# Causal mask added by VectorE in PSUM instead of by TensorE products, in a macaron transformer block

## The reference

```
q, k = rope(q), rope(k)
scores = einsum(q, k) * 64 ** -0.5
scores = where(tril, scores, -inf)
probs = softmax(scores)
out = einsum(probs, v) -> wo
```

## Time and profile before

| | |
|---|---|
| median of 3 runs | 1355.13 us (1354.36 to 1357.69) |
| profiled execution, own time | 1354.49 us |
| its span, first to last instruction | 1352.8 us |
| TensorE matmul busy | 1288.6 us, 95% |
| VectorE busy | 871.6 us, 64% |
| ScalarE busy | 618.7 us, 46% |
| GpSimd busy | 752.1 us, 56% |
| mean granted TensorE clock | 0.975 of full |

### The profile page before, as it was taken

One profiled execution on the slowest core, in us unless ns is written; L12 is line 12 of the kernel. 1 busy time (PEld: TensorE's weight loads), 2 busy tenths in 40 slices (PEclk: granted clock), 3 DMA queues, 4 the chain that ended last, 5 costly groups with the idle time before them and its releaser, 6 DMA issues. The chain is left out here.

```text
span 1352.8 us, 24949 instructions
## 1 busy us (share of the span) xinstructions
PE 1288.6 (95%) x6240; PEld 737.4 (55%) x6240; DVE 871.6 (64%) x2270; ACT 618.7 (46%) x1176; POOL 752.1 (56%) x454
## 2 busy tenths in 40 slices
PE   5986689999999999999999999999999999999798
PEld 2543455555555555555555655555555555555365
DVE  5565557767676767676767676767676767664254
ACT  3654134444444444444444444444444444444474
POOL 4123146666666656566666666666666666665300
PEclk8998599999999999999999999999999999999899
DMA  7022556555555646464646464646464646452001
GB/s 280 33 93 72 155 119 159 119 145 132 131 145 120 156 112 163 111 157 118 158 107 163 105 161 107 163 107 162 104 165 105 160 107 162 107 121 56 0 24 39
DMA packets 113612, 165.86 MB, mean 123 GB/s; under 512 B 13360, under 2 KB 63408, under 8 KB 113456
## 3 DMA queue, kind: packets, MB, share of 16 engines
q1 hardware_dynamic: 113584, 165.53, 48.0%
HBM read 37.29 MB, written 10.49 MB: 35 GB/s over the span
## 5 line engine op out<-in xcount | busy, mean ns | idle before, releaser
L862 POOL TENSOR_TENSOR psum_p<-psum_p,shared_a 128x256 f32<-128x256 f32 (+1 forms) x192 | 280.9, 1463 | 93.9 <-ACT shared_a L679 84.4
L679 ACT ACTIVATE shared_a<-bank 128x512 f32<-128x512 f32 (+3 forms) x512 | 201.5, 445 | 240.4 <-PE bank L547 232.8
L530 PE MATMUL bank<-k_hh,q_hl 128*128 128x512 f32 (+3 forms) x768 | 258.7, 392 | 9.7 <-DVE rotated L745 4.2
L547 PE MATMUL bank<-q_hm,k_l 65*128 65x512 f32 (+3 forms) x768 | 243.5, 371 | 0.0
L752 DVE TENSOR_REDUCE max_left<-bank 128x1 f32<-128x512 f32 x256 | 175.7, 687 | 93.3 <-PE bank L530 93.2
L530 PEld LDWEIGHTS bank<-k_hh,q_hl 128*128 128x128 f32 x768 | 138.1, 192 | 173.5 <-issue 72.9
L541 PE MATMUL bank<-q_hl,k_hh 128*128 128x512 f32 (+3 forms) x768 | 227.2, 349 | 0.7 <-ACT shared_a L679 0.5
L679 ACT ACTIVATE probs_more<-bank 128x512 f32<-128x512 f32 (+1 forms) x256 | 132.1, 568 | 191.1 <-PE bank L547 176.8
L756 DVE CUSTOM_DVE_ANT_0 max_scratch<-bank,tri_mask,max_left 128x128 f32<-128x128 f32 (+3 forms) x256 | 137.9, 548 | 109.6 <-PE bank L530 109.6
L567 PE MATMUL bank<-shared_a,v_cur 128*64 128x512 f32 (+3 forms) x1024 | 201.1, 471 | 0.0
L840 POOL TENSOR_TENSOR parts<-rotated,parts 128x1024 fp32r<-128x1024 f32 x64 | 152.4, 2381 | 58.0 <-ACT parts L659 58.0
(11 more groups left out here) (126 smaller groups left out, 1923.0 us busy)
## 6 DMA issues: line engine op xcount, KB each, us to landing
q_hl<-parts SPq DMA_DIRECT2D x256, 128.0 KB, 2.8
k_hh<-parts SPq DMA_DIRECT2D x256, 128.0 KB, 2.7
xn_cur<-xn_scratch SPq DMA_DIRECT2D x16, 1024.0 KB, 6.4
k_l<-parts SPq DMA_DIRECT2D x64, 256.0 KB, 4.9
q_hm<-parts SPq DMA_DIRECT2D x64, 256.0 KB, 5.0
v_cur<-shared_b SPq DMA_DIRECT2D x32, 512.0 KB, 6.0
w_qk<-w_scratch SPq DMA_DIRECT2D x32, 256.0 KB, 3.1
w_scratch<-first_w_parts SPq DMA_DIRECT2D x8, 512.0 KB, 3.1
```

The costliest lines, as they stand in the source:

```text
L530: nc.tensor.matmul(max_bank[k % 2][:, 0:w], q_hl[u][h][:, q * P:(q + 1) * P], k_hh[u][h][:, keys * CHUNK:keys * CHUNK + w], start=True, st ...
L547: nc.tensor.matmul(scores[h][:, x0:], k_l1[u][h][:, keys], q_hm[u][h][:, q], start=False, stop=True).then_inc(scores_full, 1)
L679: nc.scalar.activation(probs_of(s)[:, h, x0:], scores[h][:, x0:], ACT.Exp, scale=SCORE_SCALE).then_inc(probs_done, 1)
L862: last = nc.gpsimd.tensor_tensor(acc, acc, new, ALU.add)
```

## The change

On diagonal steps TensorE now does just high, low, high, low. VectorE then adds a [128 x 2 x 128] fp32 mask to both heads' banks with one instruction (`mask_scores`), after both low products, and both exponentials of the step wait for it through a new semaphore `masked`. For that the two score banks become one tensor. Where a diagonal step has a projection, the projection goes directly behind the scores (on VectorE its rotary work directly behind the mask). The places of the maxima, of two projections (5 to 4, 6 stays but moves in front), of the last v projection (11 to 10), and of the high and low parts (one step later) change too.

```diff
-        MAX_AHEAD = {4: (2, 3), 5: (6, 7), 6: (8, 9), 7: (11,), 8: (13,), 10: (18,), 11: (20, 21)}
-        MAX_BEHIND = {3: (0, 1), 4: (4, 5), 6: (10,), 7: (12,), 8: (14, 15), 9: (16, 17), 10: (19,), 11: (22,)}
-        MAX_LATE = (23, 24)
+        MAX_AHEAD = {3: (0, 1), 4: (2, 3), 5: (6, 7), 7: (10, 11), 9: (15,), 10: (17, 18), 11: (20, 21)}
+        MAX_BEHIND = {4: (4, 5), 6: (8, 9), 7: (12,), 8: (13, 14), 9: (16,), 10: (19,), 11: (22, 23)}
+        MAX_LATE = (24,)
-        PROJ_AT = {0: 0, 1: 1, 2: 2, 3: 3, 5: 4, 6: 5}
-        ROUND_AT, LOW_AT = {6: 0, 8: 1}, {7: 0, 9: 1}
-        V_AT = {(0, 7): 0, (0, 8): 1, (0, 9): 2, (0, 11): 3}
+        PROJ_AT = {0: 0, 1: 1, 2: 2, 3: 3, 4: 4, 6: 5}
+        ROUND_AT, LOW_AT = {7: 0, 8: 1}, {8: 0, 10: 1}
+        V_AT = {(0, 7): 0, (0, 8): 1, (0, 9): 2, (0, 10): 3}
...
-                def with_mask(h):
-                    nc.tensor.matmul(scores[h][:, x0:x0 + P], ident16[:], mask16[:], start=False, stop=False)
-
-                if s in DIAG:
-                    for part in (with_high, with_mask, with_low):
-                        for h in range(2):
-                            part(h)
-                else:
-                    for h in range(2):
-                        with_high(h)
-                        with_low(h)
+                for h in range(2):
+                    with_high(h)
+                    with_low(h)
...
                     score(p, i, u, s)
+                    if s in PROJ_AT and s in DIAG and has_next2:
+                        project(i + 1, u, PROJ_AT[s])
...
-                act.wait_ge(scores_full, 2 * NS * p + 2 * s + h + 1)
+                if s in DIAG:
+                    act.wait_ge(masked, masked_through(p, s))
+                else:
+                    act.wait_ge(scores_full, 2 * NS * p + 2 * s + h + 1)
...
+            def mask_scores(p, s):
+                x0 = first_col(s)
+                block = score_banks[:, :, x0:x0 + P]
+                dve.wait_ge(scores_full, 2 * NS * p + 2 * s + 2)
+                nc.vector.tensor_tensor(block, block, key_mask[:], ALU.add).then_inc(masked, 1)
...
                 for s in range(NS):
+                    if s in DIAG:
+                        mask_scores(p, s)
+                        if s in PROJ_AT and has_next2:
+                            rope(i + 1, u, PROJ_AT[s])
...
-        ident16, mask16 = sb("ident16", [P, P], BF16), sb("mask16", [P, P], BF16)
+        key_mask = sb("key_mask", [P, 2, P])
...
+        score_banks = ctx.enter_context(nc.psum_tensor("score_banks", [P, 2, CHUNK], F32))
+        banks = [score_banks[:, i, :] for i in range(2)]
```

More of the change, by code:

```diff
@@ L7 @@
 F32R = mybir.dt.float32r
-BF16 = mybir.dt.bfloat16
 INT32 = mybir.dt.int32
@@ L393, in attention @@
               probs_mem, v_stage, banks):
-    ones64, tri_mask, ident, ident16, mask16 = constants
+    ones64, tri_mask, ident, key_mask, score_banks = constants
     w_split, w_qk, w_v, xn_cur = ahead_of.w_out, ahead_of.w_qk, ahead_of.w_v, ahead_of.xn_cur
@@ L439, in attention @@
         max_full, max_free = sem("max_full"), sem("max_free")
-        scores_full, probs_done = sem("scores_full"), sem("probs_done")
+        scores_full, probs_done, masked = sem("scores_full"), sem("probs_done"), sem("masked")
         out_step, sum_step = sem("out_step"), sem("sum_step")
@@ L484, in sums_through, with masked_through @@
             return len(SUMS) * p + len([t for t in SUMS if t <= s])
+        def masked_through(p, s):
+            return len(DIAG) * p + DIAG.index(s) + 1
         def sums_before(p, s, back):
@@ L623, in pair @@
                             max_unit(p + 1, i + u, 1 - u, k)
-                    if s in PROJ_AT and has_next2:
+                    if s in PROJ_AT and s not in DIAG and has_next2:
                         project(i + 1, u, PROJ_AT[s])
@@ L1006, in macaron @@
         w_v = sb("w_v", [P, 2, 256], F32R)
-        banks = [ctx.enter_context(nc.psum_tensor(f"bank{i}", [P, CHUNK], F32)) for i in range(8)]
+        score_banks = ctx.enter_context(nc.psum_tensor("score_banks", [P, 2, CHUNK], F32))
+        banks = [score_banks[:, i, :] for i in range(2)]
+        banks += [ctx.enter_context(nc.psum_tensor(f"bank{i}", [P, CHUNK], F32)) for i in range(2, 8)]
         def sem(name):
@@ L1045, in _ @@
                     nc.vector.memset(ident[:], 1.0).then_inc(constants, 1)
-                    nc.vector.memset(ident16[:], 1.0).then_inc(constants, 1)
-                    nc.vector.memset(mask16[:], 0.0).then_inc(constants, 1)
+                    nc.vector.memset(key_mask[:], 0.0).then_inc(constants, 1)
                     for n in range(2):
@@ L1063, in _ @@
                 def _(pool):
[L1064 to L1069, removed]
+                    pool.wait_ge(constants, 6)
+                    nc.gpsimd.affine_select(out=ident[:], in_=ident[:], compare_op=ALU.is_equal, fill=0.0, base=0,
                                             pattern=[[1, P]], channel_multiplier=-1).then_inc(constants, 1)
+                    for h in range(2):
+                        nc.gpsimd.affine_select(out=key_mask[:, h, :], in_=key_mask[:, h, :], compare_op=ALU.is_ge, fill=MASKED,
+                                                base=0, pattern=[[1, P]], channel_multiplier=-1).then_inc(constants, 1)
                     tri = tri_mask[:, CHUNK - P:]
@@ L1074, in _ @@
                                             pattern=[[-1, P]], channel_multiplier=1).then_inc(constants, 1)
-                    pool.wait_ge(constants, 11)
+                    pool.wait_ge(constants, 10)
         weights = (*split_weights, w_down)
@@ L1084, in macaron @@
         attention(nc, x, xn_dram, xn_stored, wo_pairs, ahead, cos, sin, tables_arrived,
-                  (ones64, tri_mask, ident, ident16, mask16), shared_a, v_stage, banks)
+                  (ones64, tri_mask, ident, key_mask, score_banks), shared_a, v_stage, banks)
         macaron_half(nc, "second", x, None, None, weights, mean_of, eps_col, mem_a, mem_b, banks, None, y_t,
```

## The result

The changed kernel is slower. Eight runs of it have a median of 1364.8 us (1360.6 to 1369.4), eight runs of the kernel before 1355.2 (1352.7 to 1357.7): a ratio of 1.0075, 95% interval 1.0061 to 1.0089. The profiled execution took 1369.4 us, its span is 1367.6. The forecast was 1329, its range ended at 1349.

What follows compares the result with a forecast made beforehand. TensorE was taken as the bound in attention: 1354.5 - 45.5 (TensorE's saving) + 12 + 3.6 (VectorE's late places) + 4 (mask's wait) = 1328.6, stated as 1329 us. The 8-in-10 range was 1311 to 1349.

Steps and rivals of the forecast that it cites:

- the wait is hidden in all of them if VectorE is free at F: Diagonal steps: from F, the last low product streamed, TensorE's other work covers the mask's wait; narrow in steps 1 and 10.
- Two places are late: VectorE's queue makes TensorE wait in steps 3 and 4 (12 us) and in step 10, u = 1 (3.6 us).
- The saving on TensorE: Attention's diagonal steps: dropping 512 mask products saves 1.28 us a pair, 41.0 us over 32 pairs.
- rival 4: Whole kernel: no change, mask products were free filler beside a wait that stays; 1355 us; chance 0.05.
- The transposes: Step 6: the fp32 transpose moves behind the fp32 sums, saving 0.15 us a pair, 4.5 us over 30 pairs.
- Step 4's `project_out`: Step 4: TensorE waits for `normalise`, late in VectorE's queue; 0.4 us a pair, 12 us over 30.
- Step 10, u = 1: Maxima: unit 18 waits until VectorE has read unit 16; 0.24 us, 3.6 us over 15 pairs.
- The new wait elsewhere: Exponentials behind the mask: 3 us in the last pair, 1 us in the one before, otherwise hidden; 4 us.
- 1: Whole kernel: no new wait shows, because VectorE's lengths overlap more than laid out; 1314 us; chance 0.13.
- 2: VectorE takes back most: mask 0.69 us, not 0.43; no slack in steps 1, 10, 11; 1345 to 1355; chance 0.15.
- 3: Step 4: slower, negated maxima's transfers land late and every pair waits; 1368 to 1382 us; chance 0.07.
- 0.86 for faster: Whole kernel: chance that the change is faster, from forecast, rival without new waits and most of VectorE's; same 0.06, slower 0.08.

Runs made afterwards that it cites:

- e1: The changed kernel with 64 one-element memsets ahead of VectorE's loop, nothing inside the loop changed: 1338.6 us, ratio 0.9879 to the kernel before.
- e4: The kernel before with the new places alone (projections, maxima, v projections, high and low parts), the mask still on TensorE: 1366.9 us, ratio 1.0097.
- e3: The changed kernel without any mask add, exponentials released by the scores alone and their scale 1e-6, so the result is wrong: 1334.2 us, ratio 0.9852.
- e11: The changed kernel with 64 memsets ahead of VectorE's loop and second-half project_out moved behind step 4's values' product: 1327.5 us, ratio 0.9804.
- e5: The kernel before with the mask add on VectorE alone, every product at its old place, 64 memsets ahead of VectorE's loop: 1354.5 us, ratio 1.0003.
- e6: The changed kernel with 64 memsets ahead, second-half project_out behind step 4's values' product, and unit 23 back at step 0: 1332.5 us, ratio 0.9846.
- e8: The kernel before with 33 memsets inside VectorE's loop and 18 ahead, so the loop lies where the changed kernel's does: 1373.2 us, ratio 1.0140.

## Why the prediction was wrong

**The step that failed** is the walk of VectorE's queue: "So the wait is hidden in all of them if VectorE is free at F" and "Two places are late". I walked the queue by the lengths of its instructions and took it that an instruction can start when the one before it is done. At the return of its loop VectorE was not free at F: it was silent for 2.9 us, and the mask, the first work behind the return, started 2.0 us after its scores instead of 0.2. By e1 it costs 26 us between medians, and 31 between the two profiled executions. Of these 31, 13 returns x 1.6 us are 21, and the clock's falls cost some 8 (1.8 + 3.2 + 3.4 us for the three long pairs). I never asked what the return of a loop costs, or what 32 more instructions do to it; the trace of before showed a return of 0.3 us and no packet behind the first one, which is no bound for a longer one. Without the fetch the changed kernel takes 1338.6 us in e1: inside the 8-in-10 range, 10 above the forecast, for the reasons below.

**The saving on TensorE** was right in even pairs: e4 to e3, 36.18 to 34.93 us, is 1.25 against the forecast 1.28. In odd pairs it was 0.96, because TensorE then waits anyway, in step 10 for a maximum's bank and in step 8 for the normalised head, so that a shorter score step only makes the wait longer: rival 4's mechanism, in two steps. In all 33 us, not 41.0.

**The transposes**: step 6 in e4 is 0.16 us shorter, forecast 0.15.

**Step 4's `project_out`**: forecast 0.4 us a pair, 12 us; measured 0.31 to 0.32 in steps 4 and 5, and 10 us by the ratios of e1 and e11. Step 10, u = 1: forecast 0.24; in e3 its two products of the maxima take 0.84 us where in u = 0 they take 0.56: 0.28. In e4, with the mask on TensorE, it is 0.67 against 0.55: 0.12. The other 0.16 is the saving of that step, turned into waiting.

**The new wait elsewhere**: forecast 4 us in the last two pairs and nothing elsewhere, measured 0.9 us there and 0.1 us in each pair of the loop, 4.4 in all (e1 against e3). So the total agrees by luck. The margins of steps 1 and 10 were called narrow, and the 0.1 us a pair lies in step 10 of u = 0 and in step 11 of u = 1. In e5, with the old neighbours, the same add costs 31 us.

**Not seen**: the maximum unit 23 now comes last before the return of TensorE's own loop. Step 11 of u = 1 is 0.5 us longer than it would be (e1: 3.44, u = 0: 2.91), in 13 returns some 7 us; "issue" for 0.3 us in front of the next scores is part of it. I took the order of maxima as a queue without a seam. e6 removed this pause and lost more in steps 0 and 1, so it was not for the taking.

**The sum again**, with measured terms: 1354.5 - 33 (saving) - 4.7 (transposes) + 9.5 (`project_out`) + 1.8 (step 10, 15 x 0.12; the rest of its wait is already taken off the saving) + 4.4 (the mask's wait) + 7 (unit 23) is 1339.5, against 1338.4 for e1's profiled execution. With the fetch, 31 more: 1369.4.

**Rivals**: 1 did not happen, since `project_out` waits in step 4 of every pair. 2 named the right engine with the wrong mechanism; the mask is not longer than I took it. 3 did not happen: the view of waits has TensorE waiting for those transfers once in all the kernels, 0.6 us in e4. No rival had the return of a loop in it, and 0.86 for faster was too sure for a change that makes ScalarE wait on an engine that was 69% busy.

## What to carry to other kernels

- An edit that adds instructions to an engine's loop changes the loop's length and place: look at the instruction queue's packets and at the time from the branch to the next instruction, before and after, and before the edit is judged; a few dummy instructions ahead of the loop tell in one run whether the code's place is the cause.
- When a second engine comes between a product and its user, the places decide: the same mask add cost 31 us or 4, by what TensorE had to do next and what stood in front of the mask in VectorE's queue (these runs do not part the two). Judge such an edit together with its order, and put the first work after a loop's return where nobody waits for it.
- A pause taken out in one step is only won if the next user of the same bank or queue has slack: of four moves here (`project_out`, unit 23, the transposes, the early read) only the first kept its gain whole.

## What was not expected of the hardware

- A loop of 296 or 297 instructions on VectorE is fetched again at each of its returns at one place (457 to 753 of the program), in five packets of 8 KB an iteration, and the first instruction comes 2.9 us behind the branch (in e8 3.65, of which 3.0 are silent, behind one last pair of memsets); moved on by 32 instructions, it comes after 0.27 us with no packet.
- In the profiled execution of the changed kernel, pauses of TensorE of 1.27 to 1.58 us between stretches of full work were followed by the lower clock in 3 of 13 cases (3.4, 6.8 and 6.8 us of it, behind pauses of 1.58, 1.31 and 1.52 us), and in the other 10 by nothing; e8 with 13 pauses of 1.14 to 1.26 us shows none inside the loop.
- TensorE's first 512-wide score product behind a product in plain fp32 takes 0.34 us to the next start, where behind another score, projection or maximum it takes 0.23 to 0.24 (e1).
